# Deformable-convolution units at other steps of a pair of heads, and the causal mask as a GpSimd select

## The reference

```python
x = x + deform_conv(group_norm(x))        # 3x3, offsets from a conv, bilinear samples
t = tokens(x)                             # (8, 1024, 64)
t = t + attention(layer_norm(t))          # 16 heads of 64, rope, causal
t = t + spectral_unit(layer_norm(t))

# attention, per head
q, k = rope(q), rope(k)
att = q @ k.T / sqrt(64)
att = where(causal, att, -inf)            # the masked columns of a row end as 0
y = softmax(att) @ v
out = concat_heads(y) @ w_o.T
```

## Time and profile before

| what | us |
|---|---|
| median of 3 runs | 3895.69 |
| lowest and highest run | 3895.45 and 3910.61 |
| the profiled execution's own time | 3883.13 |
| its span, first to last instruction | 3881.3 |
| mean granted TensorE clock | 0.922 |

### The profile page before, as it was taken

One profiled execution on the slowest core, in us unless ns is written; L12 is line 12 of the kernel. 1 busy time (PEld: TensorE's weight loads), 2 busy tenths in 40 slices (PEclk: granted clock), 3 DMA queues, 4 the chain that ended last, 5 costly groups with the idle time before them and its releaser, 6 DMA issues. The chain is left out here.

```text
span 3881.3 us, 67557 instructions
## 1 busy us (share of the span) xinstructions
PE 3332.9 (86%) x20619; PEld 2283.9 (59%) x20619; DVE 2482.2 (64%) x4247; ACT 1440.9 (37%) x2188; POOL 1701.1 (44%) x1424
## 2 busy tenths in 40 slices
PE   6336999999999999999999999999999839999998
PEld 1124555555556555555565555556555528888887
DVE  2346676667666776676677667666766657474756
ACT  0001333333333333333343333333333316464545
POOL 0464555555555555555555555555655520000000
PEclk8556999899999999999999999999999969999999
DMA  2525455444544554454445544555655534343433
GB/s 78 165 85 141 120 134 132 129 119 128 134 132 119 135 140 123 116 138 132 125 126 138 137 119 123 135 137 119 139 126 130 121 81 150 101 148 103 136 115 114
DMA packets 289621, 487.64 MB, mean 126 GB/s; under 512 B 95336, under 2 KB 113144, under 8 KB 289304
## 3 DMA queue, kind: packets, MB, share of 16 engines
q1 hardware_dynamic: 257160, 398.26, 37.3%
q0 software_dynamic: 32400, 88.52, 9.4%
HBM read 258.31 MB, written 23.27 MB: 73 GB/s over the span
## 5 line engine op out<-in xcount | busy, mean ns | idle before, releaser
L1108 ACT ACTIVATE attention_probs<-attention_pss 128x896 f32<-128x896 f32 (+4 forms) x768 | 622.4, 810 | 1315.5 <-PE attention_pss L957 1304.8
L1165 DVE TENSOR_REDUCE attention_mx<-attention_pss 128x2 f32<-128x1024 f32 (+3 forms) x520 | 525.3, 1021 | 367.8 <-PE attention_pss L970 202.7
L1041 PE MATMUL attention_psY<-attention_probs,attention_xt 128*64 128x128 f32 (+7 forms) x4386 | 728.3, 438 | 2.3 <-DMA attention_xt<-xt 1.9
L1283 POOL DMA_INDIRECT attention_gat<-table,attention_idx x585 | 558.3, 954 | 191.5 <-issue 121.1
L954 PE MATMUL attention_pss<-attention_QA,attention_KA 128*128 128x512 f32 (+4 forms) x1536 | 553.4, 416 | 49.2 <-ACT attention_probs L1108 43.7
L1264 POOL TENSOR_TENSOR attention_nat_l<-attention_qk,attention_nat_h 128x512 fp32r<-128x512 f32 x260 | 425.4, 1636 | 255.4 <-ACT attention_nat_h L1127 255.4
L1704 DVE SCALAR_TENSOR_TENSOR spectral_eo<-spectral_psE,spectral_sig,spectral_eo 64x512 fp32r<-64x512 f32 x512 | 383.8, 750 | 225.5 <-ACT spectral_eo L1683 219.0
L970 PE MATMUL attention_pss<-attention_nat_h 64*128 64x512 f32 (+2 forms) x1560 | 347.5, 448 | 201.2 <-DVE attention_mx L1165 197.6
L1256 POOL TENSOR_TENSOR attention_qk<-attention_tA,attention_tB 128x512 f32<-128x512 f32 x260 | 410.9, 1591 | 205.0 <-DVE attention_tB L1180 203.6
L1607 PE MATMUL spectral_psE<-spectral_tz,spectral_up 128*128 128x512 f32 (+1 forms) x2304 | 464.7, 360 | 7.7 <-DVE spectral_eo L1704 7.5
L954 PE MATMUL attention_pss<-attention_QB,attention_KB 128*128 128x512 f32 (+4 forms) x1536 | 455.1, 352 | 0.0
(11 more groups left out here) (194 smaller groups left out, 3858.6 us busy)
## 6 DMA issues: line engine op xcount, KB each, us to landing
attention_QA<-attention_nat_h SPq DMA_DIRECT2D x520, 128.0 KB
spectral_tz<-phis SPq DMA_DIRECT2D x128, 320.5 KB, 4.6
spectral_tz<-phis SPq DMA_DIRECT2D x128, 320.0 KB, 4.3
attention_xb<-xn SPq DMA_DIRECT2D x66, 512.0 KB, 3.9
attention_wt<-wsplit SPq DMA_DIRECT2D x66, 512.0 KB, 5.9
attention_KA<-attention_nat_h SPq DMA_DIRECT2D x260, 128.0 KB
attention_KB<-attention_nat_h SPq DMA_DIRECT2D x260, 128.0 KB
attention_KA<-attention_nat_l SPq DMA_DIRECT2D x260, 128.0 KB
```

The lines of the kernel that those rows point to most:

```text
L1041: ins = pe.matmul(psY[C * half:C * half + C, c0:c1], xt[:, kt_, :], probs[:, q + c0:q + c1], start=first, stop=(j == NS - 1), skip_group_c ...
L1108: act.activation(probs[:, pstep[j]:pstep[j] + width], pss[:, slot, lead:lead + width], ACT.Exp, scale=float(E) ** -0.5).then_inc(s_act, 1)
L1165: ins = dve.tensor_reduce(mx_far[:, :, i - 4] if k0 else mx[:, :, i], scores, AX.X, ALU.max)
L1283: pool.indirect_dma_start(gat[:, n, :, :].rearrange("p q c -> p (q c)"), None, d.table.rearrange("r q c -> r (q c)"), bass.IndirectOffsetO ...
```

## The change

The units of the deformable tile move: dT to step 1 of the odd head, dR to its step 2, dX to its step 5 (behind step 4 before). On VectorE the two adds of "a" become a0 at the even head's step 3 and a1 at the odd head's step 0 (both at the even head's step 2 before), and "s" goes from the odd head's step 0 to its step 3, with three Newton rounds. The mask matmul of each key tile goes; a GpSimd `affine_select` writes zeros above the diagonal of the tile's first 128x128 block of `probs` instead, eight a head in six groups, and `pv` waits for that group's count (`s_causal`) and no longer for the exponential. The twelve groups of a pair stand at given places of `POOL_ORDER`, where the gathers stand later than before. On SyncE the residual load moves behind the copies and the load. The max units keep their mask.

```diff
--- before.py
+++ after.py
@@ -553,14 +553,14 @@
         [("rope", 2)],
         [],
         [("max", "b"), ("out",), ("rope", 3), ("max", "a")],
-        [("dT",), ("max", "c"), ("max", "d")],
-        [("max", "f"), ("dR",), ("max", "h")]],
+        [("max", "c"), ("max", "d")],
+        [("max", "f"), ("max", "h")]],
     1: [[("max", "i")],
-        [("max", "e"), ("max", "k")],
-        [("max", "j")],
+        [("max", "e"), ("max", "k"), ("dT",)],
+        [("max", "j"), ("dR",)],
         [("max", "g"), ("out",), ("row",)],
-        [("dX",)],
-        []],
+        [],
+        [("dX",)]],
 }
 
 
@@ -582,14 +582,17 @@
 
 
 HALF_STEPS = [half_steps(half) for half in range(2)]
-DEFORM_AT = {(0, 0): ["m0", "m1"], (0, 1): ["m2"], (0, 2): ["a"], (1, 0): ["s"]}
-POOL_ORDER = [("add", 0), ("add", 1), ("lower", 0), ("add", 2), ("lower", 1), ("gather", 0), ("add", 3), ("lower", 2), ("lower", 3), ("token", 0), ("gather", 1), ("token", 1), ("gather", 2)]
+DEFORM_AT = {(0, 0): ["m0", "m1"], (0, 1): ["m2"], (0, 3): ["a0"], (1, 0): ["a1"], (1, 3): ["s"]}
+POOL_ORDER = [("mask", 0), ("add", 0), ("add", 1), ("mask", 1), ("lower", 0), ("add", 2), ("mask", 2), ("lower", 1),
+              ("mask", 3), ("add", 3), ("lower", 2), ("mask", 4), ("lower", 3), ("mask", 5), ("token", 0),
+              ("mask", 6), ("gather", 0), ("mask", 7), ("gather", 1), ("mask", 8), ("mask", 9), ("token", 1), ("mask", 10),
+              ("gather", 2), ("mask", 11)]
 BODY_HEADS = 4
 UPPER_AT = {1: [0, 1], 3: [2], 5: [3]}
 SLOTS = 3
 
 
-NEWTON = 4
+NEWTON = 3
 ROOT_SEED = 1597463007.0
 
 
@@ -770,6 +773,7 @@
         s_xs = sem("xs")
         s_store = sem("store")
         s_dup = sem("dup")
+        s_causal = sem("causal")
         s_low = sem("low")
         s_ql = sem("ql")
         s_rec = sem("rec")
@@ -834,6 +838,7 @@
                 dve.sem_inc(s_def, DEF_STEPS)
                 dve.sem_inc(s_store, 64)
                 dve.sem_inc(s_sum, 2)
+                dve.sem_inc(s_causal, NS)
                 dve.sem_inc(s_H, 2)
                 dve.sem_inc(s_T, 2)
 
@@ -904,16 +909,16 @@
                         it = b * CB + c
                         for k, free, last_row in ((0, free1, row1), (1, free0, row0)):
                             pp = 1 - k
+                            wait_apart(sp, s_act, it * ACT_BODY + (ACT_AHEAD + free), s_apart)
+                            for r in range(4):
+                                copy(pp, r, 8 * it + 4 * (1 + k))
+
+                            wait_apart(sp, s_full, it * N_BODY + (N_AHEAD + roped[k]), s_apart)
+                            wait_apart(sp, s_store, 64 * it + (32 * k + 64), s_apart)
+                            load(k, (b + (c + 1) // CB) % B, ((c + 1) % CB) * 2 + k)
                             wait_apart(sp, s_full, it * N_BODY + (N_AHEAD + summed[k]), s_apart)
                             ahead = c + (1 + k)
                             residual(pp, (b + (ahead // CB + 1)) % B, (ahead % CB) * 2 + pp)
-                            wait_apart(sp, s_act, it * ACT_BODY + (ACT_AHEAD + free), s_apart)
-                            for r in range(4):
-                                copy(pp, r, 8 * it + 4 * (1 + k))
-
-                            wait_apart(sp, s_full, it * N_BODY + (N_AHEAD + roped[k]), s_apart)
-                            wait_apart(sp, s_store, 64 * it + (32 * k + 64), s_apart)
-                            load(k, (b + (c + 1) // CB) % B, ((c + 1) % CB) * 2 + k)
                             row(pp, it * ACT_BODY + (ACT_AHEAD + last_row))
                             store(k, b + ((c + 1) // CB + 1), ((c + 1) % CB) * 2 + k,
                                   DEF_STEPS * 2 * it + (DEF_STEPS * (k + 1) + (NORMED + 1)), it * DVE_BODY + (DVE_AHEAD + spread[k]))
@@ -951,11 +956,8 @@
                         for kt_, q0, c0, c1 in columns(j)[1]:
                             for a, (kt, qt) in enumerate(((KA, QA), (KB, QB))):
                                 for p0, p1 in by_bank(c0, c1):
-                                    pe.matmul(out[:, p0:p1], kt[:, h, P * kt_:P * kt_ + P],
-                                              qt[:, h, q0 + p0 - c0:q0 + p1 - c0], start=(a == 0), stop=(a == 1))
-                            d0 = c0 + P * kt_ - q0
-                            ins = pe.matmul(out[:, d0:d0 + P], identb[:, :], mask_b[:, 0, :], start=False, stop=True,
-                                            skip_group_check=True)
+                                    ins = pe.matmul(out[:, p0:p1], kt[:, h, P * kt_:P * kt_ + P],
+                                                    qt[:, h, q0 + p0 - c0:q0 + p1 - c0], start=(a == 0), stop=(a == 1))
                     elif kind == "max":
                         if u in FIRST_USE:
 
@@ -1027,7 +1029,7 @@
 
                 def pv(it, h, j, b=None):
 
-                    pe.wait_ge(s_act, it * ACT_BODY + (ACT_AHEAD + exp_read(h, j)))
+                    pe.wait_ge(s_causal, BODY_HEADS * NS * it + (NS * h + j + NS + 1))
                     if j == 0 and (h >= 0):
 
                         pe.wait_ge(s_y, BODY_HEADS * it + h + 1)
@@ -1191,11 +1193,13 @@
                         v = gat[:, 3 * x:3 * x + 3, :, :].rearrange("p k q c -> p (k q) c")
                         w = m.Wc[:, 2 * it + (k + FIRST), 3 * x:3 * x + 3, :].rearrange("p k q -> p (k q)")
                         dve.tensor_tensor(v, v, w.unsqueeze(2).to_broadcast([P, 12, C]), ALU.mult).then_inc(s_def, 1)
-                    elif op == "a":
+                    elif op == "a0":
                         v = gat[:, :, :, :].rearrange("p k q c -> p k (q c)")
-                        step.n = 3
                         dve.wait_ge(s_def, step.base + 3)
-                        step(dve.tensor_tensor(v[:, :, 0:2 * C], v[:, :, 0:2 * C], v[:, :, 2 * C:4 * C], ALU.add))
+                        dve.tensor_tensor(v[:, :, 0:2 * C], v[:, :, 0:2 * C], v[:, :, 2 * C:4 * C], ALU.add).then_inc(s_def, 1)
+                    elif op == "a1":
+                        v = gat[:, :, :, :].rearrange("p k q c -> p k (q c)")
+                        dve.wait_ge(s_def, step.base + 4)
                         dve.tensor_tensor(smp[:, :].rearrange("p (k c) -> p k c", k=K2), v[:, :, 0:C], v[:, :, C:2 * C],
                                           ALU.add).then_inc(s_def, 1)
                     else:
@@ -1272,6 +1276,14 @@
                     pool.tensor_tensor(t, t, scaled[:, buffer, :, :].rearrange("p t c -> p (t c)"),
                                        ALU.add).then_inc(s_T, 1)
 
+                def causal(j, written):
+
+                    wait_apart(pool, s_act, written, s_apart)
+                    for t in STEPS[j]:
+                        block = probs[:, poff[t]:poff[t] + P]
+                        ins = pool.affine_select(block, block, [[1, P]], ALU.is_ge, zero, base=0, channel_multiplier=-1)
+                    ins.then_inc(s_causal, 1)
+
                 def gather(x, tile, drawn, done):
 
                     if x == 0:
@@ -1288,6 +1300,7 @@
                 outs = places("out")
                 for x in range(3):
                     gather(x, FIRST, 1, None)
+                zero = pool.to_reg(0.0)
                 for kind, r in POOL_ORDER:
                     if kind == "add":
                         add(r, r + 1, 0)
@@ -1303,6 +1316,9 @@
                                     add(r, it * DVE_BODY + (DVE_AHEAD + reads_before(ORDER, place(2 * k, ("rope", r)) + 1, False)), pair)
                                 elif kind == "lower":
                                     lower(r, pair)
+                                elif kind == "mask":
+                                    h, j = 2 * k + r // NS, r % NS
+                                    causal(j, it * ACT_BODY + (ACT_AHEAD + exp_read(h, j)))
                                 elif kind == "gather":
                                     gather(r, 2 * it + (k + 1 + FIRST), 2 * it + (k + 2),
                                            DEF_STEPS * 2 * it + (DEF_STEPS * (k + 1) + 5))
```

6 lines of the change are left out of this document (3 added, 3 removed).

## The result

Measured side by side, the changed kernel takes **3739.53 us** (median of 4 runs, 3723.17 to 3749.12) against 3896.54 (3895.45 to 3910.61): a ratio of **0.958, 95% interval 0.955 to 0.961**. That is faster, and inside the range of 3490 to 3755, but 144 us above the forecast of 3595. The profiled execution took 3723.2.

What follows compares the result with a forecast made beforehand. TensorE was taken as the bound, with 64 pairs of heads at 42.95 us. Per pair -3.3 - 1.6 + 1.4 - 0.2 - 1.2 + 0.2 = -4.7 gave 38.25 us and 3595 us in all; 8 in 10 for 3490 to 3755.

Steps and rivals of the forecast that it cites:

- B: Rival: a select costs 0.65 to 0.9 us and GpSimd becomes the bound; 3720 us at 0.75; chance 0.17.
- D: Rival: holes go, clock falls as often, a mask matmul is worth only 0.04 us; 3736 us; chance 0.10.
- The two holes: TensorE's two waits a pair at max scores for VectorE's earlier reads go: -1.65 us each, -3.3 a pair.
- The select: On GpSimd: 0.45 us each, 16 a pair, 7.2 us; it fits, but only just.
- C: Rival: a select costs 1.28 us, a pair 48.2 us, the kernel is slower at 4232 us; chance 0.08.
- The mask matmuls: On TensorE: 16 mask matmuls a pair leave, 0.1 us each, -1.6 us a pair.
- The order: On TensorE: units moved to other steps keep their count, 33 a pair, nothing gained or lost.
- The clock: TensorE's granted clock: with smaller holes a third of the 1.81 us a pair lost to falls stays, -1.2.
- The SyncE edit: DMA queue: residual behind copies and load costs nothing; if copies had to wait, S0 of the next pair would.
- The gathers' new place: GpSimd's gathers start later, the last hanging 2 to 3 us into the next pair: +0.2 us a pair.
- The end of a body: S0's wait for all readers of the old loop body: 1.0 of 1.4 us kept, -0.2 a pair.
- Rival E: A new wait as large as the old ones (row transfer, dX, late select) takes all: no change; chance 0.03.

Runs made afterwards that it cites:

- moves_only: All moves and three Newton rounds against the kernel before; mask matmuls stay, no select: ratio 1.009.
- residual_first: The changed kernel with the residual load back ahead of the copies on the DMA queue: ratio 0.945 to the kernel before.
- one_gather: The changed kernel with one indirect DMA in each gather group for three, other taps left at zero: 3606 us, ratio 0.924 to the kernel before.
- resid_gather1: residual_first with the second group of gathers one select later: 3650.8 us, ratio 0.936 to the kernel before.
- dR_first: The changed kernel with dR ahead of max "j" in step 2: ratio 0.979 to the kernel before.
- gather_later: The changed kernel with the first gather group behind select 8 and the second behind the token addition: ratio 0.986 to the kernel before.
- resid_newton4: residual_first with four Newton rounds for three: ratio 0.960 to the kernel before.
- run 11: moves_only with the residual load back ahead of the copies, so mask matmuls and no select: ratio 0.995 to the kernel before.
- load_early: The changed kernel with the 1 MB load of the next operands ahead of the last rope copy: ratio 0.972 to the kernel before.
- select_only: The kernel before with only the mask as a select; old places and four Newton rounds: ratio 1.005.

## Why the prediction was right, and where it was not

The sign, the two holes and the select were foreseen; the size was not. The time lies 15 us below the upper end of the range, and that end was set by rivals B and D, neither of which happened: that the range held is luck in part. Of the prediction's own signs two failed, a pair of 38 us (40.60) and a clock above 0.97 (0.96).

**The two holes: right.** Both are gone (182.0 us in 118 waits, to 16.2 us at "h"). By the listed waits they were 182.0 / 58.7 = 3.1 us a pair, for the 3.3 of the prediction. Max "h" waits 0.26 us a pair and not 0.7.

**The select: right.** 0.37 us for 0.45, GpSimd at 29.1 us a pair for about 31, and no wait of TensorE for it. Rivals B and C are out. The multiplications' 0.6 us a pair on VectorE are not in it. Of the two rates of the Trainium skill, the GPSIMD Engine Reference's 12 cycles an element ("Elementwise — side-by-side cycle accounting") is not this instruction's: an estimate by it is 1.28 us a select.

**The mask matmuls: right in kind, a fifth too large.** One score unit with two key tiles, from its first matmul to the next unit's first; before, 1023.80 to 1024.67, with the first of these rows here; after, 1016.57 to 1017.24:

```profile
1023.80 0.39 PE L954 MATMUL attention_pss<-attention_QA,attention_KA 128*128 128x256 f32 x1
```

```profile
1016.57 0.38 PE L959 MATMUL attention_pss<-attention_QA,attention_KA 128*128 128x256 f32 x1
...
1017.24 0.97 PE L1043 MATMUL attention_psY<-attention_probs,attention_xt 128*64 128x384 f32 x6
```

That is 0.87 and 0.67: 0.10 a mask. The medians, where no wait and no half clock falls in, are 0.20 and 0.18 less for steps 1 and 2 with two masks each, but for steps 3, 4, 5 and 0 with one mask each only 0.07. A head saves 0.66, a pair 1.3, for the 1.6 taken.

**The order: not free.** "The same units with dT, dR and dX at other steps keep their count: 33 units a pair as before, nothing gained or lost." A pair's mean length less TensorE's listed waits and less half of its half clock is 37.13 us before, 37.32 in moves_only and 36.09 in the changed kernel. So the masks are worth 1.23 by this, near the 1.3, and the same units at other steps cost 0.19; together 1.04 are gained and not 1.6.

**The clock: the term that was most off in size.** Predicted -1.2 us a pair. Half clock went from 4.0 to 3.1 us a pair, and at half clock half of the time is lost, so the gain is 0.43. The reason given was a largest hole of 0.7 us. It did not hold: the row's hole is 1.34 on average and up to 1.9. One fall of the changed kernel, in windows of 4 us:

```profile
704.00:708.00 4.00, 2.79 (x21) 2.15 (x19) 0.99 (x1) 1.03 (x2) 2.56 (x5) 0.96 0.35 98
708.00:712.00 4.00, 3.50 (x17) 2.33 (x19) 3.48 (x14) 0.97 (x2) 1.28 (x1) 0.50 0.01 2
712.00:716.00 4.00, 4.00 (x19) 2.53 (x15) 1.98 (x8) 0.68 (x1) 2.94 (x4) 0.69 0.22 59
```

TensorE misses 1.2 of the first 4 us, in a row's hole of 1.71 that ends at 708.50, and then the clock is at its lower level. The mechanism itself stands: between the first and the last of the index copies the clock falls 71 times in the kernel before, each time at most 2.0 us behind a hole at L970, and 41 times in the changed one, 34 of them at the row's hole (from within it to 2 us behind it), the others at holes of 1.0 to 1.2 us. With the row's hole made smaller or removed, half clock is 1.0 (residual_first), 1.1 (one_gather) and 1.8 us (resid_gather1). Kernels with holes of another kind have as many again (5.5 in dR_first, 4.8 in gather_later, 3.1 in resid_newton4, where the wait for dX is 1.45 us each time).

**The SyncE edit: this step failed.** "I cost it at nothing; if the copies had to wait, S0 of the next pair would." The copies did not wait. But the 32 KB residual, issued 1 MB of load later and so 3 us before dR's end, makes TensorE's signals later for their readers: with the edit undone, the ratio is 0.945 for 0.958, 1.3% or about 0.8 us a pair. It costs what no wait for that transfer shows.

**The gathers' new place: the step looked at the wrong side.** It counted when gathers land (+0.2 us, and none of those waits came). It did not ask what they meet. Before, the second group starts 3.7 us behind dR's end; after, 0.1 behind it, beside the load, and max "j", dR, S3 and max "g" are read late. From them comes the row's wait, 81.7 / 62.1 = 1.32 us a pair.

**The end of a body: right, a little less.** Before, S0's wait is 40.9 us in 29 times, 1.41 each. After, it is split over the spread of the tile (L1232, 17.5 in 16), ScalarE (12.9 in 10) and five times "issue": 36.3 us in 31 times, 1.17 each. That is 0.12 a pair for the 0.2 of the prediction.

The sum of after, in the terms of the prediction: waits -0.88, clock -0.43, masks with the order -1.04, together -2.35, which is what was measured. The forecast has 2.35 us a pair too much: 1.0 in the waits (the row's 1.3, less 0.3 by which the others came out smaller), 0.8 in the clock and 0.6 in masks and order. Rival D came within 4 us of the median (3736) with the clock term at zero and masks at 0.04; neither is what happened. It was near for another reason. Rival E had a new wait as large as the old ones, which did come, though not for the row's transfer, and it took 1.3 us and not all.

**Why the parts do not add up.** The select alone is +0.5%, the moves alone +0.9%, both -4.2%. Without the moves the masks' time turns into waits for VectorE; without the selects the gathers stand back to back and the late reads are 4.1 us. Selects between them pull the groups apart. So much the runs show; the split between selects as spacers and as saved matmuls is not (run 11 has both effects).

**What stays open** is how gathers delay TensorE's signals. Shown: dR's late read vanishes with fewer gathers and nearly so with the second group further off; it shrinks with the residual elsewhere; the late reads are about 0.2, 1.0, 1.7, 2.5, 3.3, 4.1 and 4.9 us in single pairs, steps of some 0.8, and the packets of one gather take some 0.75 to land. Shown too, by the semaphore updates: the signals are held while TensorE works on. In the changed kernel those of S3 and of max "g" come a median of 0.04 us apart, where their modelled ends are 0.43 apart, and that of the output projection 0.16 behind, though its 16 matmuls take 2.00 us; in one_gather the same distances are 0.44 and 1.92. So it isn't that all three ran late. Not shown: what in a gather holds the signals, and what the load and the residual have to do with it.

## What to carry to other kernels

Moving work off the bound engine pays only together with moving what it waits for next: take the holes and the instructions out in one step, and run each alone to see which one the other needs. When a transfer or a train of gathers is moved, ask not only who waits for it, but which results of other engines are due while it is issued. If two engines are idle and the third "waits for" them, compare the end of the producer with the start of its reader before believing the list of waits; and if the trace has the signals, where they come. Here a group of gathers one select later and one 32 KB load back in its old place gave 2.3% more.

## What the hardware showed unasked

TensorE's semaphore signal can come 1.6 us behind the modelled end of a matmul (its reader up to 5.0 behind in one kernel, load_early), in the time in which indirect DMAs are issued and land; with them elsewhere it is 0.01 and the reader 0.14 to 0.23. Signals so held come in a bunch, 0.04 us apart. A 128x128 f32 affine select on GpSimd is 0.30 us alone, two back to back 0.54. With selects on GpSimd a 128x768 f32 multiplication on VectorE takes 1.56 us for 1.35, in select_only 1.57. One Newton round, 0.6 us on VectorE a pair, went with 56 us of the whole by the ratios (0.960 for 0.945, measured on two chips), more than 64 x 0.6 = 38; the wait for dX grew by 25 us and half clock from 1.0 to 3.1 us a pair, and that the round brought the latter isn't shown.
